# A transformer layer on one core: q of the second half earlier, values streaming instead of stationary, FFN groups of 4, 3, 2 and 2

## The reference

```python
# x: (4, 512, 512); H = 32 heads, D = 16
q, k, v = (x @ w.T + b).reshape(B, S, H, D)            # one w, b each
scores  = einsum('bshd,bstd->bsht', q, k) / sqrt(D)
context = einsum('bshd', softmax(scores), v)           # (B, S, 512)
x = layernorm(x + context)
dq1, dq2, dq3 = nf4_quant_dequant(w1), (w2), (w3)       # blocks of 64 along a row, 16 levels
h = silu(x @ dq1.T) * (x @ dq2.T)                      # 1376 hidden
x = layernorm(x + h @ dq3.T)
```

## Time and profile before

| | |
|---|---|
| median of 3 runs | 796.29 us (794.88 to 798.49) |
| the profiled execution | 796.93 us, span 795.1 us |
| PE busy | 730.4 us, 92% |
| weight loads | 622.8 us, 78% |
| DVE busy | 636.0 us, 80% |
| ACT busy | 483.9 us, 61% |
| GpSimd busy | 103.0 us, 13% |
| mean granted TensorE clock | 0.853 |
| DMA | 118.45 MB, 149 GB/s |

### The profile page before, as it was taken

How to read it: one execution, slowest core, us unless ns; L and a number is a source line. 1 busy time by engine, 2 the same in 40 slices (tenths; PEclk the granted TensorE clock), 3 DMA queues, 4 the chain that set the end, 5 groups by cost and what they waited for, 6 DMA issues and landing times.

```text
span 795.1 us, 14306 instructions
## 1 busy us (share of the span) xinstructions
PE 730.4 (92%) x5688; PEld 622.8 (78%) x5688; DVE 636.0 (80%) x876; ACT 483.9 (61%) x650; POOL 103.0 (13%) x97
## 2 busy tenths in 40 slices
PE   4899999964899989999799999999999999999982
PEld 4678788854899989899688877787888788888761
DVE  2799999965878898988588899999987987454386
ACT  3688979763544737546653878787666766343124
POOL 2011012102111010101011111121111111000022
PEclk9999999985555555555799999999999999999995
DMA  9964445999998694986303253201423010430347
GB/s 219 227 174 151 142 159 179 240 276 255 207 241 204 168 294 118 283 214 212 134 29 133 108 193 98 80 16 53 134 96 141 14 60 7 145 118 10 119 149 158
DMA packets 89522, 118.45 MB, mean 149 GB/s; under 512 B 24784, under 2 KB 70864, under 8 KB 86512
## 3 DMA queue, kind: packets, MB, share of 16 engines
q1 hardware_dynamic: 88320, 115.44, 51.4%
q10 hardware_dynamic: 1136, 2.10, 1.2%
HBM read 76.42 MB, written 38.86 MB: 145 GB/s over the span
## 4 chain that ended last, share of the span: by engine, by line
PE 52%; DVE 20%; issue 9%; ACT 7%; DMA 5%; SPq 5%; POOL 1%; DVEq 0%; POOLq 0%; ACTq 0%
PE ps_p L1034 10%; DVE nf_acc L1157 9%; PE ps_s L936 7%; PE ps_s L938 7%; PE ps_s L937 7%; PE ps_p L936 5%; PE ps_p L938 5%; PE ps_p L937 5%; ACT nf_y L769 4%; PE ps_s L1021 3%; PE ps_t L959 2%; DVE part L1289 2%; DMA qk_parts<-qk_p 2%; DMA k_st<-qk_parts 1%; DMA x_parts<-x_st 1%
## 5 line engine op out<-in xcount | busy, mean ns | idle before, releaser
L1157 DVE SCALAR_TENSOR_TENSOR nf_acc<-nf_y,nf_acc 128x1024 f32<-128x1024 f32 (+4 forms) x266 | 300.3, 1129 | 36.9 <-ACT nf_y L769 27.7
L769 ACT ACTIVATE nf_y<-nf_w,bound_b 128x1024 f32<-128x1024 f32 (+4 forms) x285 | 288.7, 1046 | 10.5 <-POOL nf_w L690 4.0
L1034 PE MATMUL ps_p<-probT,v_bd 128*68 128x32 f32 x1024 | 125.7, 302 | 0.0
L1034 PEld LDWEIGHTS ps_p<-probT,v_bd 128*68 128x68 f32 x1024 | 122.7, 211 | 1.4 <-DVE probT L1206 0.3
L1316 DVE TENSOR_TENSOR silu<-silu,ps_s 128x512 f32<-128x512 f32 (+1 forms) x44 | 30.1, 684 | 67.7 <-PE ps_s L938 67.7
L936 PE MATMUL ps_p<-x_hl,w_hl 128*128 128x512 f32 x192 | 77.6, 404 | 6.4 <-DVE w_hl L1175 5.0
L936 PE MATMUL ps_s<-x_hl,f_ha 128*128 128x512 f32 x192 | 75.8, 395 | 4.6 <-ACT minus_i L904 4.6
L690 POOL TENSOR_TENSOR nf_w<-nf_w,nf_rec 128x1024 f32<-128x1024 f32 (+4 forms) x19 | 39.5, 2079 | 312.2 <-DVE nf_rec L1141 312.2
L826 ACT ACTIVATE prob<-prob 128x512 f32<-128x512 f32 x32 | 20.4, 636 | 97.1 <-DVE prob L1200 97.1
L918 ACT ACTIVATE hid_hl<-silu 128x512 fp32r<-128x512 f32 (+1 forms) x44 | 27.8, 632 | 79.3 <-DVE silu L1316 79.3
L938 PE MATMUL ps_p<-x_hl,w_hl 128*128 128x512 f32 x192 | 75.5, 393 | 0.0
(11 more groups left out here) (109 smaller groups left out, 1244.7 us busy)
## 6 DMA issues: line engine op xcount, KB each, us to landing
x_hl<-x_parts SPq DMA_DIRECT2D x10, 2048.0 KB, 8.4
qk_parts<-qk_p SPq DMA_DIRECT2D x64, 204.0 KB, 2.5
q_st<-qk_parts SPq DMA_DIRECT2D x48, 272.0 KB, 6.5
k_st<-qk_parts SPq DMA_DIRECT2D x48, 272.0 KB, 7.3
x_parts<-x_st SPq DMA_DIRECT2D x16, 512.0 KB, 4.5
nf_w<-in_L_ffn_w SPq DMA_DIRECT2D x24, 256.0 KB, 3.0
dequantised<-nf_acc SPq DMA_DIRECT2D x10, 512.0 KB, 2.7
v_blocks<-v_t SPq DMA_DIRECT2D x16, 256.0 KB, 3.4
```

The source lines that it names most:

```text
L769: act.activation(nf_y[0:p, at % NY, 0:w], nf_w[0:p, u % 2, 0:w], ACT.Identity, bias=bound_b[0:p, i:i + 1], scale=STEEP).then_inc(s_ny, 1)
L1034: t = pe.matmul(ps_p[0:MV, (G + 3) % NPV, i * H:(i + 1) * H], v_bd[hb % 2][:, :, g * GI + i], probT[:, G % 2, i], start=True, stop=True)
L1157: dve.scalar_tensor_tensor(out=acc, in0=y, scalar=float(NF4[i + 1]), in1=acc, op0=ALU.min, op1=ALU.max).then_inc(s_nacc, 1)
```

## The change

- **Rooms.** `q_st1` now lies directly behind `q_st0` and `k_st0`, where `v_bd_0` was, and `v_bd_0` behind it, where weights of q and k lie in the projections. GpSimd zeroes `q_st1` at the start, zero rows are copied from there (three copies instead of four). SP loads the stacks of half block 0 one projection sooner (at 37, 39, 41 instead of 38, 40, 42) and q of half block 1 at 43, 44, 45. `v_bd_0` is cleared after product 44 (`VALUES_FREE`) and loaded after the last store of v. Only k of half block 1 waits for all projections.
- **Values.** `probT` is stationary (32 columns) and `v_bd` streams (68 columns). Product i goes to partitions 32j to 32j + 31, i = 4a + j, columns 68a on. ACT's `evacuate(G - 2)`, after `exp(G)`, copies 128 x 272 to `ctmp` (3 slots). PE's `back` transposes four 128 x 68 pieces to the old layout in one of two banks, one turn later, and `context` copies it as before, now four turns after its group and behind the first half of the levels.
- **Order.** In a turn PE takes `values` ahead of `ct`. `ct`, moments, norm and `xt` come one turn later (11 to 13, 13, 14, 15 and 16 of a block's start), so the last two `xt` of block 2 fall behind the last turn. `minus_i` is made at turn 4.
- **FFN.** Groups of 4, 3, 2 and 2. The last group has the chunks 9 and 10. A `t` turn takes two chunks only if both have 128 rows (`pairs`). `LV_F`: (2, 3) in 16 steps and (3, 3) in 12, instead of (2, 3) in 20 and (2, 2) in 13.

```diff
-    GROUPS = [range(0, 4), range(4, 8), range(8, 10), range(10, NJ)]
+    GROUPS = [range(0, 4), range(4, 7), range(7, 9), range(9, NJ)]
...
-    FIRST_STACKS = [FIRST_LOAD + 1 + 2 * k for k in range(3)]
-    FIRST_VALUES = FIRST_LOAD + 7
+    FIRST_STACKS = {FIRST_LOAD + at: which for at, which in ((0, (0, 0)), (2, (0, 1)), (4, (0, 2)),
+                                                             (6, (1, 0)), (7, (1, 1)), (8, (1, 2)))}
+    VALUES_FREE = 3 * KC * NBK - KC
...
-        LV_A[8 * b + 10:8 * b + 13] = [1, 1, 1]
+        LV_A[8 * b + 11:8 * b + 14] = [1, 1, 1]
...
-    LV_F = [(1, 2)] * 2 + [(1, 1)] * 2 + [(1, 0), (1, 2)] + [(2, 3)] * 20 + [(2, 2)] * 13
+    LV_F = [(1, 2)] * 2 + [(1, 1)] * 2 + [(1, 0), (1, 2)] + [(2, 3)] * 16 + [(3, 3)] * 12
...
+    LATE = {8 * b + 8 + k: 8 * b + 14 + k // 2 for b in range(NBK - 1) for k in range(4)}
     for G in range(GG):
-        CONTEXT_AT.setdefault(max(G + 3, LATE.get(G, 0)), []).append(G)
+        CONTEXT_AT.setdefault(max(G + 4, LATE.get(G, 0)), []).append(G)
+        BACK_AT.setdefault(G + 4 if G % 8 == 2 and G > 8 else G + 3, []).append(G)
...
+            def evacuate(G):
+                if G == 0:
+                    values_stored(act, KC * NBK)
+                act.wait_ge(s_pv, G + 1)
+                wait(act, s_back, G - NCT + 1)
+                act.activation(ctmp[:, G % NCT], ps_p[:, G % 2, 0:4 * MV], ACT.Copy).then_inc(s_evac, 1)
...
             for G in range(GG):
+                steep(LV_A[G] // 2)
                 for at in CONTEXT_AT.get(G, []):
                     context(at)
-                steep(LV_A[G] // 2)
                 exp(G)
+                if G >= 2:
+                    evacuate(G - 2)
...
-                wait(pe, s_ctx, G - NPV + 1)
+                wait(pe, s_evac, G - 1)
                 for i in range(GI):
-                    t = pe.matmul(ps_p[0:MV, (G + 3) % NPV, i * H:(i + 1) * H], v_bd[hb % 2][:, :, g * GI + i],
-                                  probT[:, G % 2, i], start=True, stop=True)
+                    a, j = divmod(i, 4)
+                    t = pe.matmul(ps_p[32 * j:32 * j + 32, G % 2, a * MV:(a + 1) * MV], probT[:, G % 2, i],
+                                  v_bd[hb % 2][:, :, g * GI + i], start=True, stop=True)
                 t.then_inc(s_pv, 1)
+            def back(G):
+                pe.wait_ge(s_evac, G + 1)
+                wait(pe, s_ctx, G - 1)
+                for a in range(4):
+                    t = pe.transpose(ps_p[0:MV, 2 + G % 2, P * a:P * a + P], ctmp[:, G % NCT, a * MV:(a + 1) * MV],
+                                     ident[:])
+                t.then_inc(s_back, 1)
...
             for G in range(GG):
                 scores(G)
+                if G >= 2:
+                    values(G - 2)
                 for key in CT_AT.get(G, []):
                     turn(key)
-                if G >= 2:
-                    values(G - 2)
+                for at in BACK_AT.get(G, []):
+                    back(at)
                 for key in XT_AT.get(G, []):
                     turn(key)
             values(GG - 2)
-            for key in TAIL_1:
+            for key in XT_AT.get(GG, []) + TAIL_1:
                 turn(key)
+            back(GG - 3)
             values(GG - 1)
             for key in TAIL_2:
                 turn(key)
+            back(GG - 2)
```

More of the change, by code:

```diff
@@ L94, in layer_kernel, with pairs @@
     NU0 = len(GROUPS[0]) + 2
+    def pairs(g):
+        js, out = list(GROUPS[g]), []
+        while js:
+            n = 2 if len(js) > 1 and rows_of(js[1]) == P else 1
+            out.append(js[:n])
+            js = js[n:]
+        return out
     def turns_of(u):
         kind, g, _ = UNITS[u]
-        return [("f", u, s) for s in range(2 if kind == "w" else -(-len(GROUPS[g]) // 2))]
+        return [("f", u, s) for s in range(2 if kind == "w" else len(pairs(g)))]
     def valid(g):
@@ L274, in layer_kernel @@
         st_0 = [sb(n, [P, H, TS], BF16, att) for n in ("q_st0", "k_st0")]
+        q_st1 = sb("q_st1", [P, H, TS], BF16, att)
         v_bd_0 = sb("v_bd_0", [P, MV, TI], F32, att)
-        st_1 = [sb(n, [P, H, TS], BF16, att) for n in ("q_st1", "k_st1")]
+        st_1 = [q_st1, sb("k_st1", [P, H, TS], BF16, att)]
         stacks = (st_0, st_1)
@@ L417, in down_over, with load_stacks @@
                 eng.wait_ge(s_down, step + 1 - n)
-        def load_stacks(eng, hb, which=range(3)):
+        def load_stacks(eng, hb, which=range(3), sides=range(2)):
             for b in which:
-                for i, terms in enumerate((Q_TERMS, K_TERMS)):
+                for i in sides:
+                    terms = (Q_TERMS, K_TERMS)[i]
                     for half in range(2):
@@ L711, in clear @@
             def clear(slot):
-                if slot:
+                if slot == 0:
+                    pool.wait_ge(s_proj, VALUES_FREE)
+                else:
                     pool.wait_ge(s_ql, 2 * KC * NBK)
@@ L726, in ones @@
                 pool.wait_ge(s_vzero[slot], 2 * Q4)
-            clear(0)
+            words = q_st1[:].rearrange("p h t -> p (h t)").bitcast(F32)
+            for q in range(Q4):
+                pool.memset(words[:, DV * TI * q:DV * TI * q + DV * TI], 0.0).then_inc(s_zero, 1)
             normalise(0)
             for tau in range(3 * KC * NBK):
-                if tau == FIRST_LOAD:
-                    pool.wait_ge(s_szero[0], 16 * 2)
+                if tau == VALUES_FREE + 2:
+                    clear(0)
                     ones(0)
@@ L881, in _ @@
             for G in range(GG):
+                steep(LV_A[G] // 2)
                 for at in CONTEXT_AT.get(G, []):
                     context(at)
-                steep(LV_A[G] // 2)
                 exp(G)
+                if G >= 2:
+                    evacuate(G - 2)
+                if G == 4:
+                    parts_stored(act, 2 * KC * NBK)
+                    values_stored(act, KC * NBK)
+                    act.wait_ge(s_ident, 2)
+                    act.activation(minus_i[:], ident[:], ACT.Copy, scale=-1.0).then_inc(s_minus_i, 1)
                 for key in XT_AT.get(G, []):
@@ L890, in _ @@
                 steep(LV_A[G] - LV_A[G] // 2)
+            context(GG - 4)
+            evacuate(GG - 2)
+            for key in XT_AT.get(GG, []) + TAIL_1:
+                high(key)
             context(GG - 3)
-            for key in TAIL_1:
-                high(key)
-            context(GG - 2)
             steep(LV_T[0])
@@ L897, in _ @@
                 high(key)
-            context(GG - 1)
+            evacuate(GG - 1)
+            context(GG - 2)
             steep(LV_T[1])
-            parts_stored(act, 2 * KC * NBK)
-            values_stored(act, KC * NBK)
-            act.wait_ge(s_ident, 2)
-            act.activation(minus_i[:], ident[:], ACT.Copy, scale=-1.0).then_inc(s_minus_i, 1)
             for s in range(NS):
@@ L913, in _ @@
                 act.activation(silu[0:rows, s % 2], ps_s[0:rows, 0], ACT.Silu).then_inc(s_silu, 1)
+                if s == 0:
+                    context(GG - 1)
                 steep(LV_F[s][0])
@@ L1111, in _ @@
                 gate_up(s)
+                if s == 0:
+                    back(GG - 1)
                 for key in F_TURNS.get(s, []):
```

81 lines of the change are left out of this document (41 added, 40 removed).

## The result

| | before | after |
|---|---|---|
| median of 4 runs | 797.39 us (794.88 to 799.38) | 831.57 us (830.13 to 833.14) |
| profiled execution, span | 796.93, 795.1 us | 833.14, 831.0 us |
| mean granted clock | 0.853 | 0.918 |

The ratio is 1.043 [1.039, 1.047]: 4.3% slower, at a higher clock. I had forecast 783 us and a range up to 809.

A forecast was written before the change was run, and what follows sets the result against it. Attention turns were taken as set by PE or an almost equally long DVE/ACT loop, the FFN by PE with DVE close behind. Terms -1.7 - 4.5 - 3.0 + 4.5 - 9.4 = -14.1 took 796.9 to 783 us; range 768 to 809.

The forecast's parts named there:

- Turns 4 to 30: Attention turns: 169.35 us would become 167.6, -1.7 us (+5 to -12), set by the DVE/ACT loop.
- the very loop above: Attention's plain turn: maximum, transpose, shift on DVE, exp and nf_y on ACT, lift; 4.88 us, growing 0.35 by evacuate.
- The product: Weights times values, 32 records on PE: 1.84 us, half of 3.68, with 0.63 and 4.6 as ends.
- the 0.98 us worked out from the rule: Values product by the skill's rule of up to 4x for 32 columns: 3.89/4 = 0.98 us.
- Strips don't overlap for f32: Rival, attention: product 3.68 us, PE sets turns, 27 turns take 188 us, total 808; chance 0.18.
- its other end, 832 us: The no-overlap rival with the weight load in the open too, a product of 4.6 us: total 832 us.
- the last rival: Clock: more streamed columns could lift the 1.2 GHz level; only attention's end gains, 778 us; no separate chance, inside first case.
- Start: Start of attention: fifth scores 2.2 us sooner for a dropped copy and 2.3 for DMA room, -4.5 us (0 to -8).
- End of attention: End of attention: 3.3 us go as minus_i is made at turn 4, other work +0.5; -3.0 us (-6 to +1).
- FFN middle: FFN steps 22 to 26: DVE falls 9.9 us behind, about 5 absorbed; +4.5 us (0 to +10).
- Behind gate/up: FFN end: two steps per block in the last group shorten 25.1 us to 15.7; -9.4 us (-7 to -11).

The follow-up runs named there:

- e3: The kernel after with rows of v_bd padded to 68 words, so streamed words lie 272 bytes apart instead of 256: 794.2 us, ratio 0.998.
- e4: The kernel after with every values product in the first strip of 32 partitions, outputs overwriting each other: 802.3 us.
- e1: The kernel before with new rooms, minus_i at turn 4 and new FFN groups, values stationary as before: 787.5 us, ratio 0.989.
- e5: The kernel before with new rooms and minus_i at turn 4 alone; old product, groups and levels: 786.9 us, ratio 0.987.
- e13: e1 (new FFN groups) with half the columns of each FFN lift left out, so weights come out wrong: 773.2 us.
- e14: e5 (old FFN groups) with half the columns of each FFN lift left out, so weights come out wrong: 783.5 us.

## Why the prediction was wrong

- **Turns 4 to 30: -1.7 forecast, +34.5 measured. The step that failed** is "ACT gets `evacuate` ... in the very loop above ... So the plain turn is 4.88 + 0.35 = 5.23 us": it took every DVE and ACT duration from rows in which the values were stationary, and priced the new product by PE's time alone. What failed was the duration of `shift`, 0.65 taken and 2.14 measured beside the product in the row above (most others 2.0 to 2.4); with the slowing gone (e3) the same loop gives 5.16. No row of before showed the stall, and none could: its four-strip product reads at 544 bytes. My range named no cost of one engine's reads to another. (By its own terms the sum of this stage was 167.9 us, not 167.6; that changes nothing.)
- **The product.** 1.84 forecast, 2.06 measured: near by luck, as a middle between two rates that didn't apply. Without the stall it is 1.21. The Trainium skill (TensorEngine Tiling (Array Packing), Performance Considerations) pairs the swap, at 32 columns, with 4 times column tiling. At the 1.2 GHz that the old product ran at, neighbouring words come to 3.4 times (3.92 to 1.14 us), 272 bytes to 3.2 and 256 bytes to 1.9, so the 0.98 us worked out from the rule are met by none of them. That neighbours do best fits the Trainium skill (Advanced Engine Details and Errata, Memory Cachelines), which penalises a new 16-byte line per access; it doesn't tell 256 from 272 bytes, which these runs do.
- **"Strips don't overlap for f32"**, the slower rival: no. e4 is nearest to that case, and it costs 175.7 us, less than the 188 I gave it, but at a granted clock of 0.98, where I had worked at 1.2 GHz. That its other end, 832 us for a product of 4.6, is the time measured is chance.
- **Clock.** It rose (0.51 to 0.77 in turns 4 to 30), as the last rival had it, and gained nothing: turns are DVE's and ACT's, and at 256 bytes the product is as long at either level.
- **Start: -4.5, measured -0.2.** What I forecast came: the fifth scores start at 192.37 instead of 196.55, 4.2 us sooner, and the first values at 182.53 (I had 183). It was lost again ahead of their maximum, which I priced at nothing. The last two records of the fourth scores start at 189.40 (181.14 before), after 3.73 us in which the profile shows nothing that PE waits for, so the maximum of turn 3 is at 189.69 instead of 185.66. From there to the maximum of turn 4 it takes 8.90 us, and 6.08 in e1, where the maximum of turn 3 is at 189.72: most of these 2.8 us are the slowing (e3, without it, has 6.41). On SP v's loads, 5.82 us, stand ahead of k's, which go out from 178.82 on. Whether that or something else holds the fourth scores isn't shown; the break stands behind their 62nd record before too, for 0.31 us, and takes 1.96 us in e1 and 6.21 in e3.
- **End of attention: -3.0, measured +0.8.** `minus_i` is gone from the path. e1 and e5 have 16.2 and 15.1 us here against 19.9, e3 18.2: so `minus_i` is worth some 4, where I had 3.3, the backs and late x1 turns cost 2 (e3 to e1) where I had 0.5, and the stall, which I didn't have, the other 2.5.
- **FFN middle: +4.5, measured +8.7.** The mechanism was right (e13 and e14 show it), the size off: PE waits 2.17 and 2.16 us for drains in steps 23 and 26, within the steps 23 to 27 that I had named. All drain waits are 1.15, 2.17, 2.16 and 1.11 us instead of 1.16 and 1.09, two waits for weights of 1.18 and 1.37 come in, together 6.9 us; the other 1.8 are not traced. I let 5 us of lag be absorbed at once; by these rows drains collect it more than once.
- **Behind gate/up: -9.4, measured -8.0**, 16.9 for 15.7 us, of which 4.8 instead of 3.6 stand ahead of the last drain. It starts 12.1 us before the end (831.0), as forecast:

```profile
818.86 0.69 DVE L1344 TENSOR_TENSOR part<-ps_p,part 128x512 f32<-128x512 f32 x1 [1.12 <-PE ps_p L976]
```

## What to carry to other kernels

Before matmuls are spread over column strips, look at the byte distance of what streams: at 256 bytes (f32) or 512 (bf16), in four strips, the product slowed DVE, ACT and GpSimd beside it here, and at 256 bytes one word of padding per row freed them. The price of a product is then not its own length but what runs beside it, so compare the mean of one unchanged instruction with and without overlap. And an instruction moved to an idle engine is only free if the two engines don't slow each other.

Of the kernels that compute the layer, e5 and e1 are the best, rooms and `minus_i` with the old product: 1.3% and 1.1% faster than before, and e5 has the old groups. With half of the FFN's lifts gone, the new groups were worth 10 us (783.5 to 773.2, single runs), so what would help next is less DVE work in the FFN.

## What was unexpected of the hardware

- Streaming at 256 bytes in four strips: 0.78 us lost per us of overlap on DVE, ACT and GpSimd; bf16 at 512 bytes 0.85 on DVE and ACT (75.1 over 88.8). At 260, 272 and 288 bytes 0.02 or less; in two strips, or at 128 bytes, 0.03.
- The length of a product of four strips at 256, 272 or 128 bytes was the same at a granted clock of 0.50 and of 1.00 (2.11 and 2.08, 1.21 and 1.19, 1.67 and 1.64 us). Only neighbouring words gained by the clock, 1.14 to 0.73.
- Weights loaded 272 instead of 256 bytes apart made the old product longer, 3.92 to 4.22 us.
- GpSimd at 1.76 us an instruction slowed DVE's two-input lifts of 1024 columns by a fifth, 1.23 to 1.49 us.
